# Four image pairs in flight in the first two convolutional attentions, and the rotation of the second stage's weights put behind them

## The reference

```python
# L0: attention over the 256 pixels of an image, then a 1x1 convolution, batch norm and relu
q, k, v = Wq x + bq (16), Wk x + bk (16), Wv x + bv (128)     # per pixel
attention = softmax(q^T k)                                     # 256 x 256 per image
out = gamma * (v attention^T) + x
x = relu(batchnorm(Wf out))
# L1: gated attention over channels
Q, K, V, Qs, Ke = W{q,k,v,s,e} x + b                           # 64, 64, 128, 16, 16 per pixel
V_dw = V * sigmoid(mean(Q * K))
attention = softmax(V_dw Qs^T)                                 # 128 x 16 per image
x = x + attention Ke
t = tokens of x                                                # pixel-major
# L2: attention with rotary positions and a top-2-of-8 mixture of experts; L3: the same kinds again
```

## Time and profile before

| | |
|---|---|
| median of 3 runs | 751.8 us (750.24 to 752.37) |
| the profiled execution | 750.25 us, span 748.4 us |
| PE busy / DVE busy / ACT busy / POOL busy | 607.8 / 577.7 / 399.6 / 155.1 us |
| the first block | from 0 to 108.6 us of the span |
| mean granted clock of TensorE | 0.778 of 2.4 GHz |

### The profile page before, as it was taken

How to read it: one execution, slowest core, us unless ns; L and a number is a source line. 1 busy time by engine, 2 the same in 40 slices (tenths; PEclk the granted TensorE clock), 3 DMA queues, 4 the chain that set the end, 5 groups by cost and what they waited for, 6 DMA issues and landing times. The chain is left out here.

```text
span 748.4 us, 9677 instructions
## 1 busy us (share of the span) xinstructions
PE 607.8 (81%) x3022; PEld 485.6 (65%) x3022; DVE 577.7 (77%) x1157; ACT 399.6 (53%) x782; POOL 155.1 (21%) x85
## 2 busy tenths in 40 slices
PE   6878977052679999999998288888885779999996
PEld 3644647041567788888887276777764758888885
DVE  2453436989876788877777789999996768999997
ACT  2212211000018788888885269999995244555553
POOL 4930002876730111111010440000000200100000
PEclk9756857666659999999999665555555589999998
DMA  3000000000013202222100000000000042222211
GB/s 136 29 0 0 0 0 1 0 0 0 1 57 121 83 27 84 85 84 84 56 1 0 0 1 1 1 0 0 0 1 26 17 138 77 78 78 77 78 56 57
DMA packets 9697, 28.80 MB, mean 38 GB/s; under 512 B 960, under 2 KB 3264, under 8 KB 9536
## 3 DMA queue, kind: packets, MB, share of 16 engines
q1 hardware_dynamic: 9664, 28.39, 11.1%
HBM read 27.21 MB, written 1.18 MB: 38 GB/s over the span
## 5 line engine op out<-in xcount | busy, mean ns | idle before, releaser
L1028 DVE TENSOR_TENSOR hL<-hraw,hH 128x1024 fp32r<-128x1024 f32 (+1 forms) x128 | 131.7, 1055 | 38.8 <-ACT hH L798 38.3
L862 PE MATMUL ps<-xH,wH 128*128 128x512 f32 x256 | 103.7, 405 | 0.0
L863 PE MATMUL ps<-xL,wH 128*128 128x512 f32 x256 | 103.1, 403 | 0.0
L864 PE MATMUL ps<-xH,wL 128*128 128x512 f32 x256 | 103.1, 403 | 0.0
L802 ACT ACTIVATE hraw<-ps,bias 128x512 f32<-128x512 f32 x128 | 86.6, 685 | 28.4 <-PE ps L864 27.8
L767 POOL TENSOR_TENSOR wL<-wraw,wH 128x1024 fp32r<-128x1024 f32 (+1 forms) x16 | 35.3, 2204 | 263.0 <-DVE wH L914 263.0
L876 PE MATMUL ps<-hH,wH 128*128 128x512 f32 x192 | 76.5, 399 | 7.7 <-DVE hL L1028 7.7
L878 PE MATMUL ps<-hH,wL 128*128 128x512 f32 x192 | 76.2, 397 | 0.0
L877 PE MATMUL ps<-hL,wH 128*128 128x512 f32 x192 | 75.9, 396 | 0.0
L798 ACT ACTIVATE hH<-hraw 128x1024 fp32r<-128x1024 f32 x64 | 67.5, 1055 | 1.0
L807 ACT ACTIVATE hraw<-ps 128x512 f32<-128x512 f32 x64 | 38.3, 598 | 51.7 <-PE ps L864 50.2
(11 more groups left out here) (211 smaller groups left out, 1286.1 us busy)
## 6 DMA issues: line engine op xcount, KB each, us to landing
G<-gates_scratch SPq DMA_DIRECT2D x32, 512.0 KB, 4.6
wraw<-in_ex SPq DMA_DIRECT2D x8, 514.5 KB, 5.4
wraw<-in_ex SPq DMA_DIRECT2D x8, 384.0 KB, 5.0
w<-in_pack SPq DMA_DIRECT2D x1, 1484.5 KB, 9.3
xs<-in_x SPq DMA_DIRECT2D x4, 256.0 KB, 3.2
out<-acc SPq DMA_DIRECT2D x4, 256.0 KB, 2.1
w<-in_pack SPq DMA_DIRECT2D x1, 492.5 KB, 3.6
gates_scratch<-gT SPq DMA_DIRECT2D x4, 32.0 KB
```

Source lines behind the costliest of these rows:

```text
L862: pe.matmul(o, wH[:, p, at:at + P], xa, start=True, stop=False)
L863: pe.matmul(o, wH[:, p, at:at + P], xb, start=False, stop=False)
L864: x = pe.matmul(o, wL[:, p, at:at + P], xa, start=False, stop=True)
L1028: dve.tensor_tensor(hL[:, k % 2, g * half:(g + 1) * half, :], src, hi.bitcast(F32), ALU.subtract).then_inc(z["hl"], 1)
```

## The change

- `L = 4` pairs are in flight, each with two PSUM banks; the hardware loop is gone, and `in_step` runs each step for pairs 0 to 3. All four pairs of images are loaded at the start, ahead of the second part of the packed weights.
- Queries and keys come from one product of 48 columns of weights (queries in rows 0 to 15, zeros, keys in rows 32 to 47). ACT adds their biases; DVE copies the values.
- `projections1` and its bias are done in two halves of two products each, since a pair has two banks; the gate's product and sum are a step of their own (`gate_sums`).
- The tokens: `attended1` makes `attention Ke` as two products of 256 columns, DVE adds `x1` (`x2`), PE transposes `x2` with four transposes a pair, and ACT copies them to `t`.
- POOL waits for all four attentions of L0 to be normalised (`m["an"] >= L`) before it turns the weights. The memset of `acc` goes to POOL's list in the experts' block, between the memset of `cmp` and the deviation; `acc` and four other tiles get their memory after the first block's is given back.

```diff
@@ loads
+            for p in range(L):
                 sp.dma_start(xs[:, p, :].rearrange("c (b n) -> c b n", b=2),
-                             a["x"][bass.ds(2 * i, 2)].rearrange("b c n -> c b n")).then_inc(m[f"xs{p}"], 16)
-            images_in(0, 0)
-            images_in(1, 1)
+                             a["x"][2 * p:2 * p + 2].rearrange("b c n -> c b n")).then_inc(m[f"xs{p}"], 16)
             sp.dma_start(w[:, early:], a["pack"][:, early:]).then_inc(s_w2, 16)
@@ POOL
             pool.wait_ge(s_w2, 16)
+            pool.wait_ge(m["an"], L)
...
-            pool.memset(acc[:], 0.0).then_inc(s_rot, 1)
+            pool.sem_inc(s_rot, 1)
@@ PE
-                pe.matmul(bank(p, 0)[0:KD], wc("Wq0"), xs[:, p, :], start=True, stop=True)
-                pe.matmul(bank(p, 1)[0:KD], wc("Wk0"), xs[:, p, :], start=True, stop=True).then_inc(m["qkp"], 1)
+                pe.matmul(bank(p, 0)[0:3 * KD], wc("Wqk0"), xs[:, p, :], start=True, stop=True).then_inc(m["qkp"], 1)
...
+            def projections1(half):
+                def step(p):
+                    pe.wait_ge(m["x1"], p + 1)
+                    if half:
+                        pe.wait_ge(m["pr"], p + 1)
+                    for c in range(2):
+                        at = (2 * half + c) * P
+                        x = pe.matmul(bank(p, c)[:, 0:272], x1[:, p, at:at + P], wc("W1"), start=True, stop=True)
...
+            def attended1(p):
+                pe.wait_ge(m["aT1"], p + 1)
+                pe.wait_ge(m["ke"], p + 1)
+                for b in range(2):
+                    x = pe.matmul(bank(p, 0)[:, b * N:(b + 1) * N], aT1[:, p, b, :], ke1[:, p, b * N:(b + 1) * N], start=True, stop=True)
+                x.then_inc(m["vp"], 1)
             def tokens(p):
+                pe.wait_ge(m["x2"], p + 1)
                 for c in range(4):
-                    o = bank(p, 3)[:, c * P:(c + 1) * P]
-                    pe.matmul(o, x1[:, p, c * P:(c + 1) * P], ident, start=True, stop=False)
-                    x = pe.matmul(o, ke1[:, p, c * P:(c + 1) * P], aT1[:, p, c // 2, :], start=False, stop=True)
+                    x = pe.transpose(bank(p, 1)[:, c * P:(c + 1) * P], x2[:, p, c * P:(c + 1) * P], ident)
@@ DVE
+            def attended1(p):
+                dve.wait_ge(m["vp"], p + 1)
+                dve.tensor_tensor(x2[:, p, :], x1[:, p, :], bank(p, 0), ALU.add).then_inc(m["x2"], 1)
-            with dve.Fori(0, 2) as j:
-                in_step((queries_keys, maxima, normalise, copy, projected1, gate, maxima1, normalise1, copy1, tokens), j)
+            in_step((values, maxima, normalise, copy, projected1(0), projected1(1), gate_sums, gate, maxima1, normalise1, copy1,
+                     attended1))
@@ POOL, in the experts' block
                 chp.done(pool.memset(cmp[:], 0.0))
+                if layer == 0:
+                    pool.memset(acc[:], 0.0).then_inc(s_rot, 1)
```

More of the change, by code:

```diff
@@ L142, in build @@
         dve_s, pool_s = sem("dve_steps"), sem("pool_steps")
-        xs = own("xs", [P, 2, CH])
+        L = B // 2
+        xs = own("xs", [P, L, CH])
         rtmp = own("rtmp", [P, B, P])
@@ L171, in build, with in_step, banks @@
         chv, chp = Chain(None, dve_s), Chain(None, pool_s)
-        def in_step(steps, j):
+        def in_step(steps):
             for step in steps:
-                for p in range(2):
-                    step(p, 2 * j + p)
+                for p in range(L):
+                    step(p)
         def bank(p, k):
-            return ps[:, 4 * p + k, :]
-        def banks(p, lo, hi):
-            return ps[:, 4 * p + lo:4 * p + hi, :]
+            return ps[:, 2 * p + k, :]
+        def banks(p):
+            return ps[:, 2 * p:2 * p + 2, :]
         @block.sync
@@ L256, in energies, with transposes @@
                 x.then_inc(m["ep"], 1)
[L258 to L261, removed]
+            def transposes(p):
+                pe.wait_ge(m["an"], p + 1)
                 for b in range(2):
@@ L264, in transposes, with fused @@
                         for c in range(2):
[L265 removed]
+                            x = pe.transpose(bank(p, b)[:, jt * N + c * P:jt * N + (c + 1) * P],
                                              A0[:, p, 2 * b + c, jt * P:(jt + 1) * P], ident)
                     x.then_inc(m["atp"], 1)
[L269 to L272 removed]
+            def fused(p):
+                pe.wait_ge(m["at0a"], p + 1)
+                pe.wait_ge(m["at0v"], p + 1)
                 for b in range(2):
@@ L278, in fused, with keys1, energies1 @@
                 x.then_inc(m["fp"], 1)
[L280 to L287, removed]
+            def projections1(half):
[6 more added lines that the diff above has]
+                        x = pe.matmul(bank(p, c)[:, 0:272], x1[:, p, at:at + P], wc("W1"), start=True, stop=True)
+                    x.then_inc(m["prp"], 1)
+                return step
+            def keys1(p):
+                pe.wait_ge(m["pr"], L + p + 1)
                 pe.matmul(bank(p, 0)[0:KD], wc("We1"), x1[:, p, :], start=True, stop=True).then_inc(m["kep"], 1)
-            def energies1(p, i):
-                pe.wait_ge(m["vd"], i + 1)
+            def energies1(p):
+                pe.wait_ge(m["vd"], p + 1)
                 for b in range(2):
@@ L320, in _, with queries_keys, exponentials @@
             act.preload_act_table(ACT.Exp)
[L322 to L327, removed]
+            def queries_keys(p):
+                act.wait_ge(m["qkp"], p + 1)
+                act.activation(q0[:, p, :], bank(p, 0)[0:KD], ACT.Identity, bias=wc("bq0", rows=KD)).then_inc(m["qk0"], 1)
+                act.activation(k0[:, p, :], bank(p, 0)[2 * KD:3 * KD], ACT.Identity, bias=wc("bk0", rows=3 * KD)[2 * KD:]).then_inc(m["qk0"], 1)
+            def exponentials(p):
+                act.wait_ge(m["nm"], p + 1)
                 for c in range(4):
@@ L352, in exponentials1, with tokens @@
                                    accum_out=sm1[:, p, b:b + 1]).then_inc(m["ex1"], 1)
-            with act.Fori(0, 2) as j:
-                in_step((values, exponentials, copy, norm_relu, gate_exp, keys1, exponentials1), j)
+            def tokens(p):
+                act.wait_ge(m["tp"], p + 1)
+                act.activation(t[:, :, 2 * p:2 * p + 2, :].rearrange("p s b c -> p b s c"),
+                               bank(p, 1).rearrange("p (b s c) -> p b s c", b=2, s=2), ACT.Copy).then_inc(m["tdone"], 1)
+            in_step((queries_keys, exponentials, copy, norm_relu, gate_exp, keys1, exponentials1, tokens))
         @block.vector
@@ L384, in normalise, with copy, projected1, step @@
                 dve.tensor_tensor(A0[:, p], A0[:, p], sm0[:, p, :, None].to_broadcast([P, 4, N]), ALU.mult).then_inc(m["an"], 1)
[L386 to L393, removed]
+            def copy(p):
+                dve.wait_ge(m["atp"], 2 * p + 2)
+                dve.tensor_copy(AT0[:, p, 2:4, :], bank(p, 1).rearrange("p (a b) -> p a b", a=2)).then_inc(m["at0v"], 1)
+            def projected1(half):
+                def step(p):
+                    dve.wait_ge(m["prp"], L * half + p + 1)
+                    dve.tensor_tensor(pr1[:, p, 2 * half:2 * half + 2], banks(p)[:, :, 0:272],
+                                      wc("bias1")[:, None].to_broadcast([P, 2, 272]), ALU.add).then_inc(m["pr"], 1)
+                return step
+            def gate_sums(p):
+                dve.wait_ge(m["pr"], L + p + 1)
                 chv.done(dve.tensor_tensor(qk1[:, p], pr1[:, p, :, 0:QK1], pr1[:, p, :, QK1:2 * QK1], ALU.mult))
```

151 lines of the change are left out of this document (70 added, 81 removed).

## The result

| | before | changed |
|---|---|---|
| median | 752.09 us (750.24 to 752.55, 4 runs) | 725.45 us (724.30 to 727.71, 4 runs) |
| ratio of the runs, 95% interval | 1 | 0.9654 (0.9625 to 0.9683) |
| the profiled execution | 750.25 us, span 748.4 | 725.55 us, span 723.7 |
| end of the first block | 108.64 us | 84.58 us |
| from there to the end of the span | 639.8 us | 639.1 us |

The change is 3.5% faster. 727 had been forecast (717 to 736), so it came out as forecast. Of the 24.7 us between the spans, 24.06 are in the first block; the rest of the kernel took what it had taken before.

A forecast was written before the change was run, and what follows sets the result against it. PE and its changing clock were taken to bound the first block, whose end every later block waits for. Its steps summed to 84.7 instead of 108.6 us, 23.9 off 750.25: 726.3, forecast as 727, range 717 to 736 (8 in 10).

The forecast's parts named there:

- Projections: Block's start on PE from 6.22 us: first pair 1.67 + 2.0, clock rising within it, three more at 0.91 + 1.09; ends 15.9.
- Tokens: Block's tail: eight 256-column products at the low clock, 6.7 us, then sixteen transposes, 3.9 us; last copy ends at 84.7.
- Energies: L0's sixteen 256-column products on PE: clock falls some 4 us in, 10.0 us, ending at 25.9.
- Normalisation undisturbed, PE idle ahead of the transposes: After L0's energies: DVE normalises four times at 1.45 us without POOL beside it, to 33.0; PE idles from 25.9 to 28.7.
- Transposes and fused products: PE after the normalisation: transposes 4 x 1.97 us to 36.6; 24 fused products, 4 low and 20 high, 12.0 to 48.6.
- Gate, with POOL beside it: DVE after L1's projections: four products and sums at 0.95 us, 3.8 together, plus 2.0 for POOL's hold; ends 62.8.
- Energies of L1 at the low clock: PE after the gate sums: 16-column products for four pairs at the low clock, 7.5 us, ending at 71.3.
- Downstream: Behind the first block: only `acc`'s 1.80 us memset is added, fitting by 0.1 us; otherwise DVE waits 0.3.
- The clock that stays high: Rival for the first block: clock high wherever PE is busy, 15.2 us less, 712; chance 0.10.
- waits in DVE's or ACT's lists: Rival for the first block: in-order steps of DVE or ACT, not PE, space the pairs; gain gone, 750; chance 0.01.
- The second rival's second half: POOL's turn holds up the gate longer, 737; first half: fused products and L1's projections run low, 742; together chance 0.08.
- The third rival: The slower case: TensorE at 1.2 GHz for the whole first block, which ends at 113.0; 755 us, chance 0.03.

The follow-up runs named there:

- e3: The changed kernel with the tokens made as before (32 products of 128 columns): ratio to before 0.9823, 736.73 us.
- e5: The kernel before with the change's new tokens alone, two pairs in flight: ratio to before 0.9847, 736.88 us.
- e4: The changed kernel with q0 and k0 padded with zeros to 128 rows for L0's energy products: ratio to before 0.9626, 721.86 us.
- e2: The changed kernel with POOL's wait moved between turned weights (now early) and turned biases (still after the normalisation): ratio to before 0.9576, 717.85 us.
- e7: The changed kernel with queries and keys as two products of 16 weight columns, into rows 0 and 32 of one bank: ratio to before 0.9682, 724.79 us.
- e10: The changed kernel with queries and keys as two products into the same rows of two banks, ahead of the values: ratio to before 0.9704, 726.89 us.
- e1: The changed kernel without POOL's wait for the four normalised attentions, so it turns weights early as before: ratio to before 0.9690, 726.6 us.

## Why the prediction was right

The total was right to 0.2%, and the mechanism at both ends of the block was as told. In the middle two terms were mis-sized, in opposite directions, and that they cancel is luck. An end in the table stands at the start of the next step where nothing lies between the two.

| step ends at | forecast | measured |
|---|---|---|
| projections | 15.9 | 16.7 |
| energies | 25.9 | 26.3 |
| last normalisation | 33.0 | 32.9 |
| transposes | 36.6 | 35.4 |
| fused products | 48.6 | 45.7 |
| L1's projections | 56.3 | 53.2 |
| gate sums | 62.8 | 62.6 |
| energies of L1 | 71.3 | 70.8 |
| `attention Ke` | 80.1 | 80.3 |
| last copy | 84.7 | 84.6 |

- *Projections.* 0.8 us late: the second pair's still took 2.6 us and only the last two 2.1 each, so the clock rose within the second pair's and not the first's.
- *Tokens.* 23 us before; 10.6 forecast, 10.8 measured, and e3 and e5 confirm the term on its own. Right.
- *Energies.* 10.0 forecast with the clock falling 4 us in; 9.6 with a fall at about 21.3, 4.6 us in. That the clock falls under a busy PE was right, and e4 shows that the sixteen rows decide it, which the forecast had only as an observation.
- *Normalisation undisturbed, PE idle ahead of the transposes.* 2.8 us forecast, 2.66 measured. Right.
- *Transposes and fused products.* Wrong in where the clock rises: I had it 3.4 us into the fused products, as before; it rose near 34.8, still in the transposes, so that all 24 fused products ran at 0.43 and PE reached the gate 3.1 us earlier.
- *Gate, with POOL beside it.* The term that was mis-sized most: 2.0 us for the hold, out of 0 to 7.1. It measured 7.22 - 1.68 = 5.5. All four products were held, since DVE came 3.1 us sooner and found 8 us of POOL's work left. The sums themselves took 0.8 us each (e2, where nothing holds them), not 0.95. So 3.1 and 0.6 us too long stand against 3.5 too short, and only by that is the end of the gate sums right to 0.2 us. I had treated the arrival and the hold as independent terms. They are one: the gate products end behind POOL's instructions, so most of PE's 3.1 us could not be gained. As a path the sum should have gone through POOL there: normalised at 33, POOL's 28.9 us, gate. That POOL would end at 62 to 64 had been forecast, and it ended at 61.9.
- *Energies of L1 at the low clock.* 7.5 forecast, 7.01 measured. Right in this kernel, and a consequence of the hold: in e2, without it, 5.49.
- *Downstream.* Right: 101.7 and 100.9 us for the next block, 538.1 and 538.2 for the rest. The memset of `acc` ended before the deviation's operand was there, by 0.1 us, the margin that the earlier trace rows had left.
- *Rivals.* The clock that stays high, the clock that stays low, the slower case and waits in DVE's or ACT's lists did not occur. The second rival's second half, POOL's turn at the gate, did in part: 5.5 of the 7.1 us on the products, and none of the 4 x 1.2 on the gates, which took 0.16 each. The third rival's price for the values, 4 x 0.73 at the low clock, is too high: the first pair's four took 2.0 us there (7.94 to 9.95 us).

## What to carry to other kernels

When work on a side engine is moved off one critical step, ask what it lies beside now, and whether the path has gone over to it. Here POOL's 29 us cost the same at either place, and cutting it in two around the sensitive step gave about 7 us. Where an engine idles and its next step starts a fixed time after another engine's start, put the sum through that engine: gains elsewhere then count only where they let it be met one instruction sooner. And where products with few rows in stand at the low clock, try padding them with zeros: it took 2.5 us off the energies and 4.1 off the tail here.

## What the runs showed of the hardware

- TensorE's granted clock fell under products with 16 rows in while the engine was fully busy: it was busy 9.2 of 9.2 us up to 21.3 us, the last 4.6 of them with these products, at 1.00, and then 4.5 of 4.5 at 0.50. It did not fall under the same products with 112 rows of zeros (6.9 us, all at 1.00, in e4). The Trainium skill (TensorE: Matmul & The Clock Gate, Part 1: The HAM clock gate) speaks of busy and idle alone.
- The clock rises under transposes too: in e2 PE had done nothing else since 29.01, and the clock was at 1.00 by 32. The Trainium skill (TensorE: Matmul & The Clock Gate, Part 4: PE-mode transpose) says that the fast clock does not engage for them; the measurement decides.
- Two fp32 products with 16 columns of weights each, the same moving operand and outputs at PSUM rows 0 and 32 start 0.01 us apart and cost as one (e7). The Trainium skill (TensorE: Matmul & The Clock Gate, Part 3: Packing small matmuls — row/col tiling) describes such packing. With the outputs in the same rows of two banks they do not overlap (e10).
- DVE and POOL locked in step lengthen each other: 1.23 to about 3.2 us on DVE's side, 2.35 to about 3.2 on POOL's (e1).
